# The two square layers of a feed-forward part computed by quarters, with seven products in place of eight

## What is computed

```python
x = x + _layernorm(attn(_layernorm(x)))
h = jax.nn.silu(_tlin(z, w1_w, w1_s)) * _tlin(z, w2_w, w2_s)     # z: layer norm of x, 256 -> 1024
h = jax.nn.gelu(_tlin(h, h1_w, h1_s), approximate=False)         # 1024 -> 1024
h = jax.nn.gelu(_tlin(h, h2_w, h2_s), approximate=False)         # 1024 -> 1024
x = x + _layernorm(_tlin(h, w3_w, w3_s))                         # 1024 -> 256
```

## Time and profile before

| | |
|---|---|
| median of 3 runs | 1233.49 us (1232.97 to 1233.98) |
| the profiled execution's own time | 1234.57 us |
| its span, first to last instruction | 1232.7 us |
| TensorE | 1193.8 us busy, 97% of the span |
| ScalarE, VectorE | 725.9 us (59%), 636.9 us (52%) |
| mean granted TensorE clock | 0.988 of full speed |
| attention's last copy of y | starts at 549.40 us |
| first matmul of the feed-forward part | 552.00 us |

### The profile page before, as it was taken

How to read it: one execution, slowest core, us unless ns; L and a number is a source line. 1 busy time by engine, 2 the same in 40 slices (tenths; PEclk the granted TensorE clock), 3 DMA queues, 4 the chain that set the end, 5 groups by cost and what they waited for, 6 DMA issues and landing times.

```text
span 1232.7 us, 17765 instructions
## 1 busy us (share of the span) xinstructions
PE 1193.8 (97%) x6705; PEld 735.9 (60%) x6705; DVE 636.9 (52%) x1211; ACT 725.9 (59%) x871; POOL 46.4 (4%) x53
## 2 busy tenths in 40 slices
PE   6789999999999989989999999999999999999998
PEld 4233333332333222338888888888888888888886
DVE  7344525452545013526647556567386475575524
ACT  6779999999999989984233242242342332423411
POOL 6001000100010000000000000000000000000000
PEclk9799999999999999999999999999999999999999
DMA  5989868986888688501101102001011011010000
GB/s 186 228 206 218 190 105 191 223 189 103 194 205 189 102 168 167 97 22 49 35 1 35 35 1 64 5 21 50 1 35 35 1 35 35 1 35 1 18 1 19
DMA packets 53483, 107.57 MB, mean 87 GB/s; under 512 B 6806, under 2 KB 23830, under 8 KB 53382
## 3 DMA queue, kind: packets, MB, share of 16 engines
q1 hardware_dynamic: 53100, 105.93, 37.0%
q10 hardware_dynamic: 288, 0.39, 0.2%
HBM read 71.62 MB, written 45.88 MB: 95 GB/s over the span
## 4 chain that ended last, share of the span: by engine, by line
PE 54%; DVE 1%; issue 0%; ACT 0%; POOLq 0%; DVEq 0%
PE ffn_ps L1661 24%; PE ffn_ps L1660 24%; PE ffn_ps L1688 2%; PE ffn_ps L1689 2%; PE side_ps L1644 1%; PE side_ps L1653 0%; DVE ln_stats L1889 0%; DVE zn L1900 0%; DVE zn L1897 0%; DVE zn L1887 0%; PE ffn_ps L1702 0%; PE ffn_ps L1703 0%; DVE ln_mean_var L1891 0%; ACT hid L1774 0%; DVE h_lo L1914 0%
## 5 line engine op out<-in xcount | busy, mean ns | idle before, releaser
L1247 ACT ACTIVATE probs<-s_ps 128x1024 f32<-128x1024 f32 x512 | 475.3, 1121 | 37.0 <-PE s_ps L1092 36.2
L1661 PE MATMUL ffn_ps<-h_lo,W 128*128 128x512 f32 x1024 | 405.9, 396 | 0.0
L1660 PE MATMUL ffn_ps<-h_hi,W 128*128 128x512 f32 x1024 | 403.0, 394 | 0.0
L1106 PE MATMUL y_ps<-probs,v_st 128*17 128x512 f32 x2048 | 273.7, 607 | 9.8 <-DVE y_sb L1272 8.8
L1774 ACT ACTIVATE hid<-ffn_ps,scales 128x512 f32<-128x512 f32 x128 | 81.0, 686 | 240.0 <-PE ffn_ps L1661 235.0
L1661 PEld LDWEIGHTS ffn_ps<-h_lo,W 128*128 128x128 f32 x1024 | 192.0, 188 | 47.5
L1660 PEld LDWEIGHTS ffn_ps<-h_hi,W 128*128 128x128 f32 x1024 | 191.9, 187 | 45.7
L1092 PE MATMUL s_ps<-q_st,k_st 50*128 50x512 f32 x1024 | 206.8, 470 | 7.9 <-DVE y_ps L1451 7.4
L1092 PEld LDWEIGHTS s_ps<-q_st,k_st 50*128 50x128 f32 x1024 | 88.3, 187 | 208.7 <-ACT probs L1247 173.7
L1920 DVE CAST h_hi<-hid 128x512 fp32r<-128x512 f32 x128 | 53.5, 418 | 192.8 <-ACT hid L1774 192.8
L1914 DVE TENSOR_TENSOR h_lo<-hid,h_hi 128x512 fp32r<-128x512 f32 x192 | 130.1, 684 | 1.1
(11 more groups left out here) (173 smaller groups left out, 892.2 us busy)
## 6 DMA issues: line engine op xcount, KB each, us to landing
k_st<-qk_scr SPq DMA_DIRECT2D x90, 128.0 KB, 6.5
q_st<-qk_scr SPq DMA_DIRECT2D x90, 128.0 KB, 7.1
w_scr<-ffn_w SPq DMA_DIRECT2D x16, 704.0 KB, 7.6
W<-w_scr SPq DMA_DIRECT2D x16, 704.0 KB, 5.9
y_scr<-y_sb SPq DMA_DIRECT2D x32, 256.0 KB, 2.5
qk_scr<-y SPq DMA_DIRECT2D x24, 256.0 KB, 7.2
qk_scr<-sums SPq DMA_DIRECT2D x24, 256.0 KB, 8.4
qk_scr<-part SPq DMA_DIRECT2D x8, 512.0 KB, 5.1
```

Source lines behind the costliest of these rows:

```text
L1106: i = pe.matmul(y_ps[32 * j:32 * j + VCOLS, :], v_st[g % 2][:, s, VCOLS * j:VCOLS * (j + 1)], probs[(PAIRS * turn + j // 2) % PROBS][:, j ...
L1247: act.activation(probs[a % PROBS][:, :, :], s_ps[a % 3][:, :, :], ACT.Exp, scale=SCALE)\
L1660: pe.matmul(bank_of(t)[:, :], w, hi[:, k, :].bitcast(form), start=(k == 0), stop=False)
L1661: mm = pe.matmul(bank_of(t)[:, :], w, lo[:, k, :].bitcast(form), start=False, stop=last)
```

## The change

A square layer Y = A B (A the weights, B the activations) is cut in quarters: A by halves of outputs and of inputs, B by halves of inputs (512) and of tokens (256). The Winograd form of Strassen's scheme takes seven products of quarters:

- C11 = A11 B11 + A12 B21
- Z = S1 T1, U2 = A11 B11 + S2 T2, U3 = U2 + S3 T3
- C21 = U3 + A22 T4, C22 = U3 + Z, C12 = U2 + Z + S4 B22

S1 to S4 are sums and differences of weight quarters, T1 to T4 of activation quarters. The change has these parts:

- **Products.** `product` has 32 matmuls of 256 columns; seven make a layer. Sums with the running result are left to PSUM where they can be: U2, U3 and C21 go into the same two banks, and ScalarE copies what is there in between (`copy_c11`, `copy_z`, `copy_u2`), for which TensorE waits. VectorE adds the copies (`add_c11`, `add_c22`, `add_c12`), and ScalarE then takes gelu in two halves of 256 columns, since rows of a quarter belong to two output tiles with scales of their own.
- **Operands.** The activations are kept in fp32 (`feed`). VectorE makes T1 to T4 in place (`make_t`), ScalarE and VectorE split each product's operand of 1024 elements a row (`high`, `low`) into a ring of three buffers.
- **Sums of weights.** In the last batch of attention, VectorE makes the 32 pieces of S1 to S4 of both layers (`sum_of_weights`, three operations each) at the turns in `SUM_TURNS`. SyncE stores each (256 KB): S1 over A21 in `W`, the others in DRAM (`sum_scr`). There are two buffers, so a sum waits until the store two before has landed. Each block of the feed-forward part then streams six operands of 1 MB from there (`stream`), into two buffers. The look at `all_exact` moves from turns 55 and 57 to 60 and 62.
- **The rest of the block.** GpSimd makes the layer norms' 1/sqrt, ScalarE the normalised values, so VectorE loses these and ScalarE the table loads for sqrt. The softmax sums are inverted once each, 64 a row, before they are spread by DMA (four reciprocals of 256 columns go). TensorE's list in the feed-forward part becomes a loop as well.

The core of the diff:

```diff
 W_ALL = W3_AT + HT * DIM
+LAYERS, HK, HM = 2, HT // 2, HIDDEN // 2
+HB = BLK // 2
+SUM_KINDS = ("S3", "S1", "S2", "S4")
+SUM_UNITS = LAYERS * HK * len(SUM_KINDS)
+STREAMED = ("S2", "S3", "S4")
+SUM_TURNS = (2, 3, 4, 5, 6, 7, 10, 11, 12, 13, 14, 18, 19, 20, 21, 22, 23, 25, 27, 29, 31, 37, 41, 42, 45, 47, 48, 52, 54,
+             56, 58, 59)
 W_CHUNK = W_ALL // QUADS
...
+            def store_sum(j):
+                l, kt, kind = j // 16, j % 16 // 4, SUM_KINDS[j % 4]
+                if kind == "S1":
+                    dst = quarter_of_w(l, kt, 1, 0)
+                else:
+                    dst = sum_scr[len(STREAMED) * l + STREAMED.index(kind), :, kt * HM:(kt + 1) * HM]
+                sp.wait_ge(sum_made, j + 1)
+                sp.dma_start(dst, qk[j % 2][:, :]).then_inc(sum_stored[j % 2], 16)
...
+                if t in SUM_TURNS:
+                    store_sum(SUM_TURNS.index(t))
...
+            def sum_of_weights(j):
+                l, kt, kind = j // 16, j % 16 // 4, SUM_KINDS[j % 4]
+                a11, a12, a21, a22 = (quarter_of_w(l, kt, m, k) for m, k in ((0, 0), (0, 1), (1, 0), (1, 1)))
+                dst, prior = qk[j % 2][:, :], qk[1 - j % 2][:, :]
+                if j >= 2:
+                    dve.wait_ge(sum_stored[j % 2], 16 * (j // 2))
+                if j:
+                    dve.wait_ge(sum_made, j)
+                    dve.wait_ge(sum_checked, 2 * j)
+                else:
+                    dve.wait_ge(v_stored, 16 * PROJECTED)
+                if kind == "S3":
+                    dve.tensor_tensor(dst, a11, a21, ALU.subtract).then_inc(sum_made, 1)
+                elif kind == "S1":
+                    dve.tensor_tensor(dst, a21, a22, ALU.add).then_inc(sum_made, 1)
+                elif kind == "S2":
+                    dve.tensor_tensor(dst, prior, a11, ALU.subtract).then_inc(sum_made, 1)
+                else:
+                    dve.tensor_tensor(dst, a12, prior, ALU.subtract).then_inc(sum_made, 1)
+                dve.wait_ge(sum_made, j + 1)
+                bits = v_aug[:, :, :, :, :].rearrange("p q t j n -> p (q t j n)")[:, 0:HM].bitcast(I32)
+                dve.tensor_scalar(bits, dst.bitcast(I32), LOW_BITS, None, ALU.bitwise_and).then_inc(sum_checked, 1)
+                dve.wait_ge(sum_checked, 2 * j + 1)
+                dve.tensor_reduce(w_bits[:, 2 * QUADS + j:2 * QUADS + j + 1], bits, AX.X, ALU.max).then_inc(sum_checked, 1)
...
-        bank = [ctx.enter_context(nc.psum_tensor(f"ffn_ps{a}", [P, BLK], F32)) for a in range(BANKS)]
+        feed = [sb(f"feed{l}", [P, 4, 2, BLK], F32) for l in range(LAYERS)]
+        RING = 3
...
+        PRODUCTS = ("A11 B11", "A12 B21", "S1 T1", "S2 T2", "S3 T3", "A22 T4", "S4 B22")
+        NP = len(PRODUCTS)
+        K_C11, K_C11_END, K_Z, K_U2, K_U3, K_C21, K_C12 = range(NP)
+        PRODUCT_BANKS = (BANKS_X, BANKS_Y, BANKS_Z, BANKS_X, BANKS_X, BANKS_X, BANKS_Z)
+        Q11, Q12, Q21, Q22 = range(4)
+        OPERAND_AT = (Q11, Q21, Q11, Q11, Q12, Q21, Q22)
...
+            def stream(i, n):
+                l, k = n // 3, (K_U2, K_U3, K_C12)[n % 3]
+                old_l, old_k = (n - 2) % 6 // 3, (K_U2, K_U3, K_C12)[(n - 2) % 3]
+                old_i = i if n >= 2 else i - 1
+                if not (isinstance(old_i, int) and old_i < 0):
+                    sp.wait_ge(tile_done, tile_at(old_i, old_l, old_k, 1))
+                sp.dma_start(sums[n % 2][:, :, :].rearrange("p k m -> p (k m)").bitcast(F32), sum_scr[n])\
+                    .then_inc(sums_loaded[n % 2], 16)
...
-                for k in range(HT):
-                    if done_before is not None:
-                        pe.wait_ge(h_lo_done, done_before + k + 1)
-                    for m in ms:
-                        if k == 0:
-                            wait_bank(pe, i, t0 + m)
-                        tile(i, t0 + m, w_at, width, m, [(k, k == HT - 1)], hi, lo)
...
+                elif k == K_U2:
+                    pe.wait_ge(copied, copied_at(i, l, 0, h))
+                elif k == K_U3:
+                    pe.wait_ge(copied, copied_at(i, l, 2, h))
...
+            def product(i, l, k):
+                slot, fresh = (NP * l + k) % RING, k in (K_C11, K_C11_END, K_Z)
+                pe.wait_ge(op_lo_done, op_at(i, l, k))
+                if k in (K_U2, K_U3, K_C12):
+                    n = 3 * l + (K_U2, K_U3, K_C12).index(k)
+                    pe.wait_ge(sums_loaded[n % 2], 16 * (3 * i + n // 2 + 1))
+                for h in range(2):
+                    wait_product_bank(i, l, k, h)
+                    dst = bank[PRODUCT_BANKS[k][h]]
+                    for kt in range(HK):
+                        cols = slice(kt % 2 * HB, (kt % 2 + 1) * HB)
+                        for a in range(2):
+                            w = weights(l, k, kt, 2 * h + a)
+                            for part in (op_hi, op_lo):
+                                mm = pe.matmul(dst[:, a * HB:(a + 1) * HB], w, part[slot][:, kt // 2, cols].bitcast(form),
+                                               start=(fresh and kt == 0 and a == 0 and part is op_hi),
+                                               stop=(kt == HK - 1 and a == 1 and part is op_lo),
+                                               skip_group_check=not fresh)
+                    mm.then_inc(tile_done, 1)
...
+            def step(i, u, ahead):
+                if not is_zero(i):
+                    pe.wait_ge(x2_lo_done, i)
+                for t in range(2 * HT):
+                    first_tile(i, t)
+                for k in range(NP):
+                    product(i, 0, k)
+                    if ahead and k == K_U2:
+                        project_y(i)
+                for k in range(NP):
+                    product(i, 1, k)
...
-            def each_block():
-                for i in range(BLOCKS):
-                    step(i, i % 2, i + 1 < BLOCKS, i > 0)
...
+                blocks(step, pe.Fori)
...
+            def high(i, o):
+                wait_operand(i, o)
+                wait_slot(i, o)
+                act.activation(op_hi[o % RING][:, :, :], operand(o), ACT.Copy).then_inc(op_hi_done, 1)
...
+            def copy_u2(i, l, h):
+                act.wait_ge(tile_done, tile_at(i, l, K_U2, h))
+                act.activation(feed[1 - l][:, Q12, h, :], bank[BANKS_X[h]][:, :], ACT.Copy).then_inc(copied, 1)
...
+                    normalise(Z, i + 1, zn, zn, z_norm)
+                high(i, 12)
+                copy_u2(i, 1, 0)
+                copy_u2(i, 1, 1)
+                high(i, 13)
...
+            def low(i, o):
+                dve.wait_ge(op_hi_done, OPS * i + o + 1)
+                dve.tensor_tensor(op_lo[o % RING][:, :, :], operand(o), op_hi[o % RING][:, :, :].bitcast(F32), ALU.subtract)\
+                    .then_inc(op_lo_done, 1)
+            def make_t(i, l, n):
+                b11, b12, b21, b22 = (feed[l][:, q, :, :] for q in range(4))
+                if n == 1:
+                    if l:
+                        dve.wait_ge(gelu_done, gelu_at(i, 0, Q12, 1))
+                    else:
+                        dve.wait_ge(prod_done, HT * i + HK)
+                    dve.wait_ge(op_lo_done, op_at(i, l, K_C11))
...
+            def add_c22(i, l, h):
+                dst = feed[1 - l][:, Q22, h, :]
+                dve.wait_ge(copied, copied_at(i, l, 1, h))
+                dve.wait_ge(tile_done, tile_at(i, l, K_U3, h))
+                dve.tensor_tensor(dst, bank[BANKS_X[h]][:, :], dst, ALU.add).then_inc(added, 1)
```

More of the change, by code:

```diff
@@ L92 @@
     scales: object
+    signs_p: object
     ident: object
@@ L1018, in _ @@
             store_y(HALVES - 1)
+            for slot in range(2):
+                sp.wait_ge(sum_stored[slot], 16 * SUM_UNITS // 2)
         @block.gpsimd
```

900 lines of the change are left out of this document (558 added, 342 removed).

## The result

The changed kernel takes 1245.21 us (median of 5 runs, 1239.36 to 1247.70); the kernel before takes 1233.49 us (5 runs, 1231.34 to 1236.57). The ratio is 1.0082, 95% interval 1.0055 to 1.011: **slower by 0.8%**, where 1228 us and faster was forecast. 1245 us lies inside the stated range of 1204 to 1248, but on the other side of the old time.

What follows compares the result with a forecast made beforehand. TensorE was taken to bound the kernel, busy 97% of the span. From the profiled 1234.6 us, -54.1 + 15.1 + 33.5 = -5.5 gave 1229.1 us; the median, 1.1 us lower, was forecast at 1228 us, range 1204 to 1248.

Steps and rivals of the forecast that it cites:

- The products: Feed-forward layers: 224 matmuls at 0.1182 us replace 128 at 0.2333, 3.4 us less a layer, -54.1 us over sixteen.
- The sums of weights: Last batch of attention: VectorE's sums wait for stores queued behind loads, making copies of y late, +33.5 us.
- The stalls inside a block: Feed-forward part: TensorE waits for ScalarE, VectorE, first streamed loads and loop jumps, +15.1 us, bounds 4 to about 35.
- copy of U2, seven blocks: Second layer: TensorE's third product into one bank waits 1.0 us for ScalarE's copy of U2, in each of seven blocks.
- add of C22, six blocks: First layer: C21 waits about 0.6 us for VectorE's add of C22, in each of six blocks.
- first block's few loads: First block: VectorE waits for small softmax-sum loads queued behind two 1 MB streams, costing TensorE 3.5 us.
- jumps: TensorE's new feed-forward loop: three entries or jumps of 0 to 2.7 us, taken as 1 us in all.
- the walk: Second layer: step-by-step addition of VectorE's and ScalarE's times, reaching 16.1 us against TensorE's 15.1 us of products.
- E: The end of the first layer's last product, from which the second layer's steps were timed.
- The chain of ScalarE and VectorE: Rival, chance 0.20: in the blocks instructions do not overlap, 3.5 us more a block, 25 us in all, 1253 us.
- Prompt stores: Rival, chance 0.15: stores of sums land promptly in attention, which then costs 6 us, total 1200 us.
- The third: Rival, chance 0.03: feed-forward matmuls of 256 columns miss their price, 188 ns each, time over 1400 us.

Runs made afterwards that it cites:

- the kernel without the gaps: Changed kernel with C22 adds, U2 copy, last split and x1 statistics and normalisation reordered, and TensorE's feed-forward list unrolled: 1223.31 us, ratio 0.9921.

## Why the prediction was wrong

**The products: right.** -54.1 us was forecast. 128 matmuls at 0.1168 and 96 at 0.1197 make 26.4 us a layer, 3.4 us less than 29.87: -54.9 us.

**The sums of weights: right.** +33.5 us was forecast, +32.9 measured, 34.2 by the medians with and without the sums. The single steps: 20.7 us for the group before the copy of turn 9 (35.34 instead of 14.67; +21.6 forecast), +0.3 for the next (-1.0), +10.6 for that before turn 25 (+11.0), +1.3 for the one after (+1.9). In the first the store landed 27.5 us after the copy of turn 1 (28.8 forecast) and the four sums took 7.8 us (7.5). The runs, made in this order, split the sum in 14.3 us of queue, 15.2 us of two buffers and 3.3 us of the rest.

**The stalls inside a block: the step that failed.** The term was +15.1 us; from the first matmul on, the part gained 25.0 instead of 39.0 us, and with the products as measured that is +29.9 us. By its pieces:

| | forecast | measured in the profiled execution |
|---|---|---|
| copy of U2, seven blocks | 7.0 | 13.8, with 0.7 in the last block's first layer |
| add of C22, six blocks | 3.6 | 5.1 |
| first block's few loads | 3.5 | 0: VectorE had them 8.3 us into the block |
| jumps | 1.0 | 3.8 |
| low part of y, seven blocks | 0 | 2.9 |
| end of the last block | 0 | 1.3 (15.4 instead of 14.1 us for its output tiles) |

The rest, 3 us, is in restarts and the projection. In the U2 chain the walk was of the right steps, but with steps that were too small; in the output tiles and the low part of y there was no walk. The walk put the restart behind the copy of U2 at E + 16.1; with E at 625.38 us it came at 642.37, E + 17.0. ScalarE's timeline shows the steps:

```profile
635.21 1.71 ACT L2005 ACTIVATE feed<-feed,scales 128x256 f32<-128x256 f32 x4 [1.89 <-DVE feed L2146]
636.83 1.04 ACT L1976 ACTIVATE op_hi<-feed 128x1024 fp32r<-128x1024 f32 x1
637.78 1.05 ACT L1988 ACTIVATE feed<-ffn_ps 128x512 f32<-128x512 f32 x2
638.73 2.07 ACT L2011 ACTIVATE zn<-zn,ln_shift,ln_rstd 128x256 f32<-128x256 f32 x4
640.70 1.04 ACT L1976 ACTIVATE op_hi<-feed 128x1024 fp32r<-128x1024 f32 x1
641.64 1.06 ACT L1992 ACTIVATE feed<-ffn_ps 128x512 f32<-128x512 f32 x2
```

Four normalisations take 1.97 us and four half gelus 1.62, where I had 1.4 for each: 0.49 and 0.40 us a step, not the estimated 0.35. VectorE's part, too, was 0.4 us longer: this list starts at E + 9.8, not E + 9.4. The splits of 1024 columns start 0.95 us apart, as the walk had them, and the copies with the restart were 0.3 us shorter. The half-row steps were among the numbers that the text called its weakest. A margin of -1 became one of -1.95, since in a chain that is already over, each 0.1 us that a step is longer is 0.1 us of TensorE, seven times.

**A loss that no term had.** The forecast took the profiled execution as typical, 1.1 us above the median. After the change it was 5.9 us below. The 2 us gaps and the jumps are at times followed by stretches at half the clock, and the price of a gap is then 3.5 us and not 2. That the 5.9 us are such stretches is argued from the mean clocks and from the kernel without the gaps, not read from a trace of the slower runs. The rows had one such stretch, 0.50 at 459 us, behind a stall of TensorE, and I used it for attention alone.

**The sum.** The profiled execution was forecast at 1229.1 us and took 1239.4. Stalls give +14.8 of the difference, products -0.8, sums -0.6, and attention up to turn 1 ran 3.1 us shorter here (421.85 against 424.92 us), with 0.2 at the entry: +10.5, within 0.2 us. No term had the 3.1 us, and they are luck at least in part: this copy starts anywhere between 421.3 and 424.6 us in the traces of the changed kernel and its edits. Another 7.0 us are the median against the profile.

**The rivals.** The chain of ScalarE and VectorE was given 0.20 and 1253 us; steps longer than the walk had are what came, though not for its reason: it had instructions that do not overlap, and the splits overlap as before. The two chains lost 18.9 us where 10.6 was forecast, about 1 us a block more, which is where it was to decide; all stalls together lost 1.9 us a block more. Prompt stores fell with the first wait of 23.1 us. The third fell with 0.1168 us. The page "TensorE: Matmul & The Clock Gate" of the Trainium skill (section Back-to-back issue gap) would have had the right sign by the wrong step: its estimate made a layer 5 us longer, and a layer is 3.4 us shorter without its stalls, 1.6 us shorter with them (25.0 over 16).

## What to carry to other kernels

Where a change takes an engine from a large margin to none, every wait in its new list is to be walked with the steps of the very shapes it has; a step estimated 0.1 us short counts once per pass. A wait removed by a move in an in-order list is only removed when what stood behind the moved piece has been followed to its last reader; here the wait for the copy of U2 took four moves. And a helper's DMA that a busy engine waits for needs its own queue and enough buffers before its bytes are counted as free.
